# Two steps of a mixture-of-experts hand-over moved into the stage before it

## What is computed

```
x = x + attention_0(layernorm(x), ctx)                  # stage A
s = layernorm(x) @ Wr.T + br
w = softmax(s);  idx = top_k(s + biases, 2)             # stage A: router
val = w[idx] / sum(w[idx])
h = layernorm(x) @ Wl1[e] + bl1[e];  a, b = halves(h)   # stage B, e in idx
y_e = (silu(a) * b) @ Wl2[e] + bl2[e]
x = x + sum over the 2 experts of val_e * y_e           # start of stage C
x = x + attention_1(layernorm(x), ctx);  x = x + conv_ffn(layernorm(x))
```

## Time and profile before

| | us |
|---|---|
| median of 3 runs | 981.99 (980.72 to 982.06) |
| the profiled execution | 982.82 |
| its span, first to last instruction | 981.0 |
| stage A (to the start of B's first work) | 0 to about 212.5 |
| stage B | about 212.5 to 440 |

### The profile page before, as it was taken

One profiled execution on the slowest core, in us unless ns is written; L12 is line 12 of the kernel. 1 busy time (PEld: TensorE's weight loads), 2 busy tenths in 40 slices (PEclk: granted clock), 3 DMA queues, 4 the chain that ended last, 5 costly groups with the idle time before them and its releaser, 6 DMA issues. The chain is left out here.

```text
span 981.0 us, 26151 instructions
## 1 busy us (share of the span) xinstructions
PE 880.1 (90%) x8788; PEld 747.0 (76%) x8789; DVE 593.8 (61%) x1484; ACT 467.1 (48%) x1194; POOL 386.9 (39%) x606
## 2 busy tenths in 40 slices
PE   5888888669999999989999899999999999679995
PEld 4676767439999999977474888888888887468784
DVE  3587877545545555531126566867768668349995
ACT  3787887413222222212334444444444544359894
POOL 4488886610000000007002554546545463436662
PEclk9999999879999999999999999999999999879997
DMA  6445547342433333316963899798997977312111
GB/s 168 122 150 168 195 146 235 121 176 59 126 99 104 97 96 93 94 38 215 333 214 127 170 200 197 147 188 188 176 185 154 202 164 139 69 39 62 58 57 44
DMA packets 222058, 137.78 MB, mean 140 GB/s; under 512 B 160288, under 2 KB 207392, under 8 KB 221856
## 3 DMA queue, kind: packets, MB, share of 16 engines
q1 hardware_dynamic: 180304, 99.78, 40.3%
q10 hardware_dynamic: 38608, 28.65, 11.4%
q0 software_dynamic: 3072, 8.39, 2.7%
HBM read 81.79 MB, written 54.98 MB: 139 GB/s over the span
## 5 line engine op out<-in xcount | busy, mean ns | idle before, releaser
L1737 ACT ACTIVATE c_pT<-c_T 128x512 f32<-128x512 f32 (+2 forms) x90 | 50.2, 595 | 101.8 <-PE c_T L1896 71.5
L1686 POOL TENSOR_TENSOR c_soft<-c_soft,c_share 128x616 f32<-128x616 f32 (+2 forms) x96 | 70.4, 761 | 62.6 <-DVE c_share L2149 61.1
L1079 ACT ACTIVATE b_rowsT<-b_RT 128x256 f32<-128x256 f32 x39 | 15.0, 385 | 157.9 <-PE b_RT L1121 157.9
L1696 POOL MEMSET d_round<- 128x1 f32 x1 | 0.1, 99 | 227.0 <-POOLq L969 227.0
L1193 DVE COPY b_w<-moe_w 128x1024 f32 x78 | 53.6, 689 | 53.0 <-issue 47.6
L1130 PEld LDWEIGHTS b_G<-b_rowsT,b_w 128*128 128x128 f32 x624 | 77.2, 195 | 4.5 <-DVE b_w L1193 2.1
L1130 PE MATMUL b_G<-b_rowsT,b_w 128*128 128x128 f32 x624 | 77.9, 279 | 1.7 <-ACT b_rowsT L1079 0.9
L1207 DVE SCALAR_TENSOR_TENSOR b_hidT<-b_U,b_bias,b_gate 128x128 f32<-128x128 f32 x156 | 43.9, 344 | 55.3 <-PE b_U L1130 55.3
L1130 PE MATMUL b_U<-b_rowsT,b_w 128*128 128x128 f32 x624 | 76.5, 276 | 0.0
L1157 PE MATMUL b_Y<-moe_w,b_hidT 128*128 x312 | 73.9, 380 | 0.9 <-DVE b_out L1238 0.9
L1130 PEld LDWEIGHTS b_U<-b_rowsT,b_w 128*128 128x128 f32 x624 | 73.3, 193 | 0.0
(11 more groups left out here) (239 smaller groups left out, 2128.7 us busy)
## 6 DMA issues: line engine op xcount, KB each, us to landing
rel_windows<-c_relw ACTq DMA_DIRECT2D x28, 368.0 KB, 7.5
c_bias<-rel_windows SPq DMA_DIRECT2D x16, 616.0 KB, 6.5
prob_rows<-c_soft SPq DMA_DIRECT2D x16, 616.0 KB, 7.7
moe_w<-in_L_Wl SPq DMA_DIRECT2D x16, 512.0 KB, 3.9
early<-in_L_early SPq DMA_DIRECT2D x16, 384.0 KB, 3.2
values<-c_pT ACTq DMA_DIRECT2D x22, 256.0 KB, 3.3
b_rows<-expert_lists SPq DMA_DIRECT2D x39, 128.0 KB, 2.1
expert_out<-b_out SPq DMA_DIRECT2D x39, 128.0 KB, 1.7
```

The costliest lines, as they stand in the source:

```text
L1686: ins = nc.gpsimd.tensor_tensor(soft[p][:, hs, a:z], soft[p][:, hs, a:z], share[:, s, hs].unsqueeze(2).to_broadcast([P, HS, z - a]), ALU.mult)
L1737: nc.scalar.activation(dst, view(T[k]), ACT.Copy, **kw).then_inc(g["emptied"], 1)
```

## The change

It has these parts:

1. **The zeroing comes one batch earlier.** `places` of batch 14 now also forms the totals; a new DVE step `list_ends`, ahead of `list_rows(14)`, writes `count_i` from them. The rows behind the list as it stands without batch 15 are zeroed: 256 rows, since batch 15 adds at most 128. So each DMA writes 256 KB instead of 128 KB.
2. **SP alone zeroes**, all 8 experts, ACT none.
3. **`scatter` of batch 15 waits on POOL** until all 8 have landed, since it writes over zeroed rows.
4. **`places(15)` on PE** comes ahead of the text values of step 18 (half 3).
5. **SP loads the rows of tiles 0 and 1 in stage A**: after `tile_row` is there (new semaphore `s_tiles`), and for the rows themselves after all zeroing and all scatters have landed. Their buffers move to `shared`; in stage B the loads of tiles 0 and 1 fall away. SP's two text stores come behind these loads.
6. **SP no longer waits at the end of stage A** for the landing of text stores (nor for the zeroing, on SP or ACT); DVE waits for all four in stage B, ahead of the second `up_weights`.

```diff
-        def pad(eng, first):
+        def pad(eng):
             eng.wait_ge(s_count, 1)
-            for e in range(first, NE, 2):
-                n = eng.value_load(count_i[0:1, e:e + 1], min_val=0, max_val=NB * P)
-                eng.dma_start(t["lists"][bass.ds(n + e * ROWS_E, P)], zeros[:, :]).then_inc(s_pad[first], 16)
-
-        def padded(eng, first):
-            eng.wait_ge(s_pad[first], 16 * NE // 2)
+            for e in range(NE):
+                n = eng.value_load(count_i[0:1, e:e + 1], min_val=0, max_val=NE * ROWS_E - 2 * P)
+                eng.dma_start(t["lists"][bass.ds(n, 2 * P)].rearrange("(p o) d -> p o d", o=2),
+                              zeros[:, :].unsqueeze(1).to_broadcast([P, 2, D])).then_inc(s_pad, 16)
...
             by_batch(steps)(sp)
-            pad(sp, 0)
+            pad(sp)
+            sp.wait_ge(s_tiles, 1)
+            for p in range(2):
+                row = sp.value_load(shared["tile_row"][0:1, p:p + 1], min_val=0, max_val=NE * ROWS_E - P)
+                if p == 0:
+                    sp.wait_ge(s_pad, 16 * NE)
+                    for q in range(2):
+                        sp.wait_ge(s_sc[q], 32 * (NB // 2))
+                sp.dma_start(shared["rows"][p][:, :], t["lists"][bass.ds(row, P)]).then_inc(shared["s_rows"][p], 16)
             for n in range(EARLY_HALVES - 4, EARLY_HALVES - 2):
                 text_store(sp, n, text_dv, n - 3)
-            padded(sp, 0)
-            for out in shared["s_text_out"][:2]:
-                sp.wait_ge(out, 16 * EARLY_HALVES // TEXT_BANKS)
...
             def scatter(b, p):
+                if isinstance(b, int) and b == NB - 1:
+                    pool.wait_ge(s_pad, 16 * NE)
...
             by_batch(steps)(act)
-            pad(act, 1)
             text_values(range(EARLY_HALVES - 2, EARLY_HALVES))
             exp_scores()
-            padded(act, 1)
...
-                if isinstance(b, int) and b == NB - 1:
+                if isinstance(b, int) and b >= NB - 2:
                     dst = T[1][:, D + 2 * NE:D + 3 * NE]
...
+                if isinstance(b, int) and b == NB + 2:
+                    places(b - 3, 1 - p)
                 if isinstance(b, int) and b >= NB:
                     text_values(text_halves(b))
-                if isinstance(b, int) and b == NB + 2:
-                    places(b - 3, 1 - p)
...
+            def list_ends(b):
+
+                if isinstance(b, int) and b == NB - 2:
+                    dve.wait_ge(g["pos_mm"], b + 1)
+                    nc.vector.tensor_copy(count_i[:, :], T[1][:, D + 2 * NE:D + 3 * NE]).then_inc(s_count, 1)
...
                 if lists:
+                    list_ends(b - 4)
                     list_rows(b - 4, p)
...
-            nc.vector.tensor_copy(count_i[:, :], count[:, :]).then_inc(s_count, 1)
...
-            nc.vector.tensor_copy(shared["tile_row"][:, :], tr[:, :])
+            nc.vector.tensor_copy(shared["tile_row"][:, :], tr[:, :]).then_inc(s_tiles, 1)
...
-                load(n, p)
+                if not isinstance(n, int) or n >= 2:
+                    load(n, p)
...
             for p, e in enumerate((e_out, e_ahead)):
                 gate_weights(p, p, e)
                 bias_columns(p, p, e)
+                if p == 1:
+                    for out_copy in shared["s_text_out"]:
+                        dve.wait_ge(out_copy, 16 * EARLY_HALVES // TEXT_BANKS)
                 up_weights(p, p, e)
             dve.wait_ge(g["bias_sb"], 2)
             hidden(0, 0)
-            for out_copy in shared["s_text_out"][2:]:
-                dve.wait_ge(out_copy, 16 * EARLY_HALVES // TEXT_BANKS)
             combine()
```

More of the change, by code:

```diff
@@ L256, in layer0 @@
         s_sc = [sem(f"a_scatter{p}") for p in range(2)]
-        s_pad = [sem(f"a_pad{k}") for k in range(2)]
+        s_pad = sem("a_pad")
+        s_tiles = sem("a_tiles")
         s_count = sem("a_count")
@@ L983, in experts @@
         tile_expert, tile_row = shared["tile_expert"], shared["tile_row"]
-        rows = [sb(f"b_rows{p}", [P, D]) for p in range(2)]
+        rows = shared["rows"]
         rowsT = [sb(f"b_rowsT{p}", [P, KD, P]) for p in range(2)]
@@ L1006, in experts @@
         s_clear = sem("b_clear")
-        s_in = [sem(f"b_in{p}") for p in range(2)]
+        s_in = shared["s_rows"]
         s_out = [sem(f"b_out_{p}") for p in range(2)]
@@ L2581, in build @@
             "short": sb("short_context", [P, KD * NB * NSHORT]),
+            "rows": [sb(f"first_rows{p}", [P, D]) for p in range(2)],
+            "s_rows": [ctx.enter_context(nc.semaphore(f"s_rows{p}")) for p in range(2)],
             "s_text_out": [ctx.enter_context(nc.semaphore(f"s_text_out{k}")) for k in range(TEXT_BANKS)],
```

## The result

The changed kernel took 982.65 us (median of 22 runs, 980.22 to 985.39), the kernel before, run in turn with it, 979.19 (22 runs, 976.82 to 982.81). The ratio is 1.0037, 95% interval 1.0027 to 1.0046: slower by 0.37%, some 3.5 us, where 0.6 us less had been forecast. The 981.99 from which the forecast counted was a median of three and lies 2.8 us above that of the 22; its profiled execution, 982.82, is as slow as the slowest of them. So it is luck that 982.65 falls inside the stated range of 979.2 to 984.2: the forecast had the time going down, and it went up.

What follows compares the result with a forecast made beforehand. PE is busy 90% of the span, but only the boundary of stages A and B was taken to matter: barrier +1.0, rows -1.7, b_U +0.1, net -0.6 us, from 981.99 to 981.4 us; range 979.2 to 984.2.

Steps and rivals of the forecast that it cites:

- The rows' 1.7 us: Start of stage B: rows loaded in stage A let b_G start 1.7 us sooner after the barrier.
- POOL's slack: End of stage A: POOL's three us before the barrier (211.4 - 208.5) are used up, and 1.0 more.
- places(15) earlier: PE, end of stage A: gains nothing; half 3 and the rest end 1.3 us later, hidden behind POOL.
- pitch of the zeroing: SP's eight zeroing DMAs: 1.21 us from one to the next, bounds 1.13 and 1.30; the last at 203.0.
- POOL's wait: Last scatter waits for all zeroing: starts at 205.6, POOL's drain ends at 212.4, barrier +1.0 us.
- Rival 3: Zeroing on SP's queue bound by its transfers, late by eight times the excess over 1.21 us; slower by over 0.2%; 15%.
- its example of 1.65: Zeroing on one queue: if crossing text halves and scatters make one write hold it 1.65 us, time is 984.9 us.
- Landing to scatter: POOL, end of stage A: all zeroed at 205.3, last scatter starts 0.3 us later, at 205.6.
- SP behind the scatter: SP, end of stage A: scatter lands at 209.4, then two row loads, two text stores and drain, done at 211.95.
- b_U at the low clock: PE, stage B, behind b_G: 2.41 us at mostly the low clock, starting earlier with more slow stretch: +0.1 us.
- half 3 at 3.76 us: PE's text values, end of stage A: half 3 taken as 3.76 us; with the rest it ends at 209.4 instead of 208.1.
- rival 1: Barrier: POOL's drain is absorbed, SP last at 211.95, net -1.1, 980.9 us; with the forecast 70%.

Runs made afterwards that it cites:

- e4: Kernel before with parts 5 and 6 alone (zeroing stays at the end, on SP and ACT): ratio 0.9960 to the kernel before (0.9939 to 0.9981).
- e6: Kernel before with part 6 alone (no wait for text stores in stage A, zeroing still waited for): ratio 0.9998 to the kernel before (0.9972 to 1.0024).
- e2: Changed kernel with places(15) put back behind half 3 on PE: ratio 1.0035 to the kernel before (1.0013 to 1.0057).
- c1_before: Kernel before, unchanged, profiled a second time: half 3 took 1.96 us, against 3.76 in the first profile; no ratio given.
- c2_after: Changed kernel, unchanged, profiled a second time: barrier opened 20.3 us after the scatter of batch 14, 19.6 expected; no ratio given.

## Why the prediction was wrong, point by point

**Right.** The rows' 1.7 us: from the barrier's opening (the L137 events) to b_G it takes 3.4 in all three profiles of the changed kernel and in e4, against 5.2 and 5.1 before. DVE's weights release b_G, and b_G runs at half clock (3.78). DVE's new wait in stage B costs nothing up to the first b_hidT (e6). POOL's slack is used up by the new wait, and its drain, 2686 ns in every profile, moves with it. places(15) earlier gains nothing, and its delay of PE stays hidden as long as the zeroing is last (e2).

**Wrong: the term "pitch of the zeroing".** The prediction took 1.21, with 1.30 as the upper bound, from an issue of 0.34 plus at most an estimated 0.09 for twice the pieces. The form of the DMA (256 pieces of 1 KB from a broadcast source) made it 0.572, and the pitch (205.3 - 195.2)/7 = 1.44: 1.6 us over seven. With the first issue 0.2 late (its register load took 0.824) the last one goes out 9.6 after the scatter of batch 14 where 7.8 was computed. The bound was extrapolated from another form of DMA, and it was the one number that counted seven times. (Its lower end has a slip: 1.21 with register loads shorter by 0.10 is 1.11, not 1.13; nothing hangs on it.) This is the step that failed: at the pitch of 1.21 that it took, POOL's wait would have cost the barrier 1.0, less than the rows gave. Rival 3 had the right place, but named the transfers as the cause; they land in a steady 2.5 us each and don't queue. It was the issue. Its formula with the measured 1.44 gives 1.8 more, +1.2 in all, which is about the size of this term; its example of 1.65 was not reached.

**Wrong, smaller.** Landing to scatter 0.1 more; SP behind the scatter 0.8 more than the 5.05 computed from its second DMA to SP's drain (second load of rows 1.5 after the first, not 1.15; text stores 0.4), so that SP, not POOL, is last, 0.4 later than POOL would be; b_U at the low clock for longer (2.86 instead of 2.41), so 0.5 more from b_G to b_hidT instead of 0.1 more. Together: -0.6 + 1.8 + 0.1 + 0.4 + 0.4 = +2.1, and D differs by +2.0. That accounts for this pair of profiles; in c2_after the same D is split otherwise.

**Wrong: the profile it was set against.** The other 1.5 us of the 3.5 are not in that pair. The prediction read half 3 at 3.76 us as the kernel's property; it was one state of the clock. Half 3 stood ahead of places(15) and so of the barrier, and with the clock up it is 1.8 us shorter and starts 0.7 earlier (c1_before). The changed kernel can't have that gain, since its barrier hangs on a fixed chain of issues. In the six profiles of kernels with the zeroing at the end the last scatter came 4.1 (three times), 5.2, 5.7 and 6.5 after that of batch 14, 4.9 in the mean. With 21.1 to 21.6 from there to b_hidT that makes a D of about 26.3, an estimate, and the changed kernel's 30.1 is 3.8 more: near the +3.5 of the medians. But six profiles are few, and an execution's whole time varies by more than that; so the mixture as the cause of the other 1.5 is argued, not shown.

**The rules weighed.** By the Trainium skill, page "DMA: Bandwidth & Descriptors", section "Latency and other measured facts", a register load has a floor of about 600 ns; here the shortest was 262, the median 340, the first and longest of the eight 824, so the measurement decides against it as a floor. POOL's drain took 2686 ns in all thirteen profiles, also where POOL had idled 9.4 us ahead of the last scatter, which settles rival 1: it is not absorbed. The Trainium skill, page "PSUM — Partial Sum Buffer", section "Engine vs sequencer instructions", says that a drain waits for the engine to go fully idle; with nothing shown on POOL during the 2.686 us, the traces bear that out only if POOL was busy with something that they don't show.

## What to carry to other kernels

Work moved off the end pays only if what now waits for it is later than its own finish: count the whole chain, number of issues times pitch, then whoever waits, then that engine's drain. Where a duration counts many times, take it from a DMA of the same form, not the same size. And look whether a long instruction on the path stood at the low clock: one profile shows one of several lengths (1.96 to 3.76 us for half 3 here), and a second profile of the same kernel is the cheapest experiment there is. Where the clock differs, start the ruler behind the place where it differs.

## What the runs showed of the hardware

A DMA issue on SP took 0.572 us as 256 pieces of 1 KB with a broadcast source and 0.340 as 128 pieces of 2 KB, for the same 256 KB; which of the two differences counts was not separated. POOL's drain at the end of stage A took 2.686 us in all thirteen profiles, whatever POOL had waited for before it. The four products of half 3 took 1.96 us at full clock and 3.76 at half, in two profiles of the same kernel, and 3.10 to 3.44 in three others in which the clock was low for part of them.
